# A fused S6, MoE, S5, MoE kernel: four small moves in its order by slots

## The reference, cut to what matters

```
x = x + S6(layernorm(x))       # 8 x 512 x 128; selective scan, 256 channels x 64 states
x = x + MoE(layernorm(x))      # 8 experts, hidden 256, top 2, all experts computed
x = x + S5(layernorm(x))       # diagonal complex scan, 64 states
x = x + MoE(layernorm(x))      # the same weights again

S6:   h[t] = exp(delta[t] * A) * h[t-1] + (delta[t] * x[t]) * B[t];  y[t] = C[t] * sum(h[t])
MoE:  logits = x @ Wg; the two largest, softmax over them -> combine
      out = sum_e combine[e] * ((silu(x @ W1[e]) * (x @ W2[e])) @ W3[e])
S5:   xs = scan with Lambda_bar = exp(Lambda * step); y = Re(C xs) + D * u
```

## Time and profile before

| | |
|---|---|
| device time, median of 3 runs | 1831.92 us (1828.08 to 1833.31) |
| the profiled execution | 1833.74 us, span 1831.9 us |
| mean granted TensorE clock | 0.866 |
| busy: VectorE, GpSimd, TensorE, ScalarE | 84%, 82%, 74%, 69% of the span |
| `h` scans on VectorE | 1024, mean 1210 ns, 1191.1 us busy |
| `w` products on GpSimd | 512, mean 2360 ns, 1192.4 us busy |

### The profile page before, as it was taken

How to read it: one execution, slowest core, us unless ns; L and a number is a source line. 1 busy time by engine, 2 the same in 40 slices (tenths; PEclk the granted TensorE clock), 3 DMA queues, 4 the chain that set the end, 5 groups by cost and what they waited for, 6 DMA issues and landing times. The chain is left out here.

```text
span 1831.9 us, 19041 instructions
## 1 busy us (share of the span) xinstructions
PE 1348.5 (74%) x5928; PEld 612.4 (33%) x5928; DVE 1535.7 (84%) x2154; ACT 1264.5 (69%) x2227; POOL 1497.5 (82%) x876
## 2 busy tenths in 40 slices
PE   5336468678866888778876887768876878668958
PEld 1001123234332433224332343324332343225525
DVE  3999988988899888998999888998999888995232
ACT  4558568777877678786886868777777777664413
POOL 0999989879998799978998899977998899984212
PEclk9556679888998989889897989989898989889969
DMA  3511411131113211122111310132101401100000
GB/s 117 192 52 50 165 46 52 50 123 67 58 47 104 89 52 52 49 92 98 58 46 56 137 52 29 55 109 98 50 32 50 164 29 49 46 29 1 6 1 6
DMA packets 38747, 121.89 MB, mean 67 GB/s; under 512 B 5875, under 2 KB 21110, under 8 KB 26358
## 3 DMA queue, kind: packets, MB, share of 16 engines
q1 hardware_dynamic: 37062, 120.67, 18.5%
q10 hardware_dynamic: 1584, 0.01, 0.0%
HBM read 109.13 MB, written 11.53 MB: 66 GB/s over the span
## 5 line engine op out<-in xcount | busy, mean ns | idle before, releaser
L1275 DVE TENSOR_TENSOR_SCAN h<-da,w 128x512 f32<-128x512 f32 x1024 | 1191.1, 1210 | 111.2 <-ACT da L853 94.5
L956 POOL TENSOR_TENSOR w<-ur,br 128x1024 f32<-128x1024 f32 x512 | 1192.4, 2360 | 29.9 <-DVE h L1275 17.5
L853 ACT ACTIVATE da<-dr,al 128x511 f32<-128x511 f32 x1024 | 680.8, 686 | 245.0 <-DVE h L1275 242.9
L646 PE MATMUL ys<-h,wsum 128*32 128x512 f32 x2048 | 315.4, 692 | 186.7 <-DVE h L1275 167.4
L580 PE MATMUL bankH<-nT,w 128*128 128x512 f32 x512 | 304.5, 679 | 98.5 <-DVE aq L1199 92.8
L899 POOL TENSOR_TENSOR x<-x,yk 128x512 f32<-128x512 f32 x120 | 152.5, 1271 | 181.4 <-ACT yk L815 181.4
L592 PEld LDWEIGHTS bankY<-w,aq 128*128 128x128 f32 x2048 | 250.6, 195 | 85.4 <-issue 75.8
L592 PE MATMUL bankY<-w,aq 128*128 128x128 f32 x2048 | 258.1, 280 | 12.4 <-DVE aq L1199 7.9
L580 PE MATMUL bankG<-nT,w 128*128 128x512 f32 x432 | 249.8, 662 | 16.4 <-DVE aq L1199 16.4
L815 ACT ACTIVATE yk<-bankY,rt 128x128 f32<-128x128 f32 x480 | 140.8, 360 | 86.6 <-PE bankY L592 77.5
L580 PEld LDWEIGHTS bankH<-nT,w 128*128 128x128 f32 x512 | 86.4, 203 | 258.0 <-DVE aq L1199 165.1
(11 more groups left out here) (188 smaller groups left out, 1156.0 us busy)
## 6 DMA issues: line engine op xcount, KB each, us to landing
br<-b_rows SPq DMA_DIRECT2D x64, 1024.0 KB, 5.0
dr<-d_rows SPq DMA_DIRECT2D x16, 1024.0 KB, 7.4
ur<-u_rows SPq DMA_DIRECT2D x16, 1024.0 KB, 8.4
d_rows<-vh SPq DMA_DIRECT2D x16, 256.0 KB
u_rows<-th SPq DMA_DIRECT2D x16, 256.0 KB
xnew<-in_L_attn_a_x_dram SPq DMA_DIRECT2D x8, 256.0 KB, 5.3
w<-in_L_ffn_W_dram SPq DMA_DIRECT2D x2, 1024.0 KB, 11.1
x<-in_L_attn_a_x_dram SPq DMA_DIRECT2D x8, 256.0 KB, 9.0
```

Of the source, the lines that this page charges most:

```text
L646: ins = nc.tensor.matmul(ys[32 * q:32 * q + 32, :], wsum[:, :], h[:, (DUOS * b + 2 * group + q // 2) % H_RING, q % 2, :], start=(n == 0), ...
L853: A(da[duo % D_RING][:, k % 2, 1:L], dr[:, half, q, 1:L], ACT.Exp, scale=nega[:, QUADS * half + q, n:n + 1]).then_inc(decay_ready, 1)
L956: G.tensor_tensor(w[:, turn_duo % W_RING, :, :], ur[:, half, q:q + 2, :], br[:, chunk % B_RING, row:row + 1, :].to_broadcast([128, 2, L]), ...
L1275: V.tensor_tensor_scan(h[:, turn_duo % H_RING, k % 2, :], da[duo % D_RING][:, k % 2, :], w[:, turn_duo % W_RING, k % 2, :], 0.0, ALU.mult, ...
```

## The change

Four moves of order; no instruction is added or taken away.

1. `x1T` goes from slot 26 in bank Y to slot 25 in bank G, and `h1_0` waits until it is drained.
2. `lg1` and `lg2` go a slot later (28 to 29, 105 to 106), and so do tiles `h_2` and `h_3` of both MoEs, so the logits stand behind `h_0` and `h_1`. R1 to R4 follow by their lags.
3. VectorE's S5 rotation, scan and rotation back go a slot later; TensorE's slots and line 1252's stay.
4. Ahead of turn 0 the S5 matrices are built (VectorE) and turned (TensorE) before `delta` is made, and the copy of the spread rows (line 1013) goes behind it.

```diff
+    if j in (2, 3) and step == 0:
+        return at + 1
...
-SETUP_ROWS_AT = PRE_AT + 9
-SETUP_AT = PRE_AT + 17
-MATRICES_AT = PRE_AT + 17
+SETUP_ROWS_AT, ROWS_AT = PRE_AT + 9, PRE_AT + 17
+SETUP_AT = PRE_AT + 11
+MATRICES_AT = PRE_AT + 10
...
-    (5, "post", "Y", "z"), (MOE_AT[1] - 2, "post", "Y", "x1T"), (MOE_AT[1], "post", "Y", "lg1"),
+    (5, "post", "Y", "z"), (MOE_AT[1] - 3, "post", "G", "x1T"), (MOE_AT[1] + 1, "post", "Y", "lg1"),
...
-    (MOE_AT[2] - 2, "post", "Y", "x3T"), (MOE_AT[2], "post", "Y", "lg2"),
+    (MOE_AT[2] - 2, "post", "Y", "x3T"), (MOE_AT[2] + 1, "post", "Y", "lg2"),
...
+                        if name == "h" and n == 0:
+                            pe.wait_ge(drained[BANK[turned]], t.before(turned) + 1)
...
+                yield ROWS_AT
                 v.wait_ge(rows_spread, 1)
                 chain(V.tensor_copy(bcs[:, :, :].rearrange("p n c -> p (n c)"), ys[:, 0:3 * D]))
...
-                yield SLOT["P1"] + 1
+                yield SLOT["P1"] + 2
                 p1, p2 = got(t, "P1"), got(t, "P2")
...
-                yield SLOT["P1"] + 5
+                yield SLOT["P1"] + 6
                 drain("P2", V.tensor_tensor(zt[1], p2[:, :], sinT[:, :], ALU.mult))
```

More of the change, by code:

```diff
@@ L167, in moe_pe @@
 def moe_pe(m, late):
-    return sorted(([] if late else [(MOE_AT[m], "lg", 0)]) + [(SLOT[f"h{m}_{j}"], "h", j) for j in tiles_in(m, late)]
+    return sorted(([] if late else [(SLOT[f"lg{m}"], "lg", 0)]) + [(SLOT[f"h{m}_{j}"], "h", j) for j in tiles_in(m, late)]
                   + [(SLOT[f"g{m}_{j}"], "g", j) for j in tiles_in(m, late)]
@@ L561, in moe @@
                 c = t.b - 1
-                lnk = {1: 2, 2: 4}[m]
+                lnk, turned = {1: 2, 2: 4}[m], f"x{2 * m - 1}T"
                 if not is_late:
@@ L1237, in post @@
                 V.tensor_tensor(p2[:, :], p2[:, :], sinT[:, :], ALU.mult).then_inc(sin_ready, 1)
-                yield SLOT["P1"] + 2
+                yield SLOT["P1"] + 3
                 v.wait_ge(drained[BANK["P1"]], t.before("P1") + 1)
@@ L1241, in post @@
                 V.tensor_tensor(p2[:, :], zt[2], p2[:, :], ALU.add).then_inc(turned_ready, 1)
-                yield SLOT["P1"] + 3
+                yield SLOT["P1"] + 4
                 v.wait_ge(turned_ready, c + 1)
                 V.tensor_tensor_scan(p2[:, :], rT[:, :], p2[:, :], 0.0, ALU.mult, ALU.add).then_inc(diagonal_scanned, 1)
-                yield SLOT["P1"] + 4
+                yield SLOT["P1"] + 5
                 v.wait_ge(diagonal_scanned, c + 1)
                 V.tensor_tensor(zt[0], p2[:, :], cosT[:, :], ALU.mult).then_inc(real_ready, 1)
-                yield SLOT["P1"] + 5
+                yield SLOT["P1"] + 6
                 drain("P2", V.tensor_tensor(zt[1], p2[:, :], sinT[:, :], ALU.mult))
```

## The result

The changed kernel takes 1878.26 us (median of 4 runs, 1877.65 to 1878.66) against 1832.62 of the kernel before (4 runs, 1828.08 to 1842.61): ratio 1.0241, 95% interval 1.0199 to 1.0283. The forecast was 1850.7 and its range ended at 1857. It is slower, as forecast, but by 46 us in place of 19.

The account below looks back on a forecast made before the run. Neither VectorE nor GpSimd is full; a turn's length is VectorE's work plus its waits. Terms 0 + 6.3 - 0.7 + 11.2 + 2.0 + 0 = +18.8 gave a median of 1850.7, range 1832 to 1857.

Parts of the forecast that it names:

- the first claim: Whole turn: a wait saved or added on VectorE carries through; 2.3 of the 2.8 us between turns 5 and 6.
- Start: Ahead of turn 0: an earlier first scan only lengthens later waits for products; 0, bounds -5.2 and 0.
- a sign of being wrong: Start-up: GpSimd's first product ahead of 46 would show the forecast wrong.
- rival D: Start-up: the 5.2 us are kept, 1845.5, if the first product comes sooner; chance 0.04.
- Rotation: S5: waits of 1.0, 1.1 and 0.3 replace 1.43; +1.05 per turn, +6.3 over turns 1 to 6, -0.7 in turn 7.
- Second MoE, start: Second routing, turns 1 to 7: tiles end 0.9 later and R3 adds 0.7; 7 x 1.6 = +11.2.
- The wait at slot 109: Second MoE: sign of being right, this wait grown to over 2, with R3 right behind the following `aq`.
- R3's 0.7: Second MoE: R3 leaves the wait of 1.97, stands behind its scan and delays the next by 0.7 us per turn.
- First MoE: First routing: +0.65 in turns 2, 4, 6 and 0 in turns 1, 3, 5, 7; sum +2.0.
- The wait of 1.2 for a product at slot 30: First MoE: sign of being right, a new wait of about 1.2 where R1 had filled the gap.
- End: After turn 7: same work, earlier rows against later logits; 0, bounds -1 and +1.
- Rival E: Both routings: TensorE at full clock, -0.6 x 7 at the second MoE; 1828.9, not slower; chance 0.08.

Follow-up runs that it names:

- fill_gap3: The changed kernel with 3 matmuls of zero weights ahead of the first tile of the first MoE's fourth quartet: 1856.86 us, ratio 1.0133.
- only_start: The kernel before with only the S5 matrices made ahead of `delta`: 1839.95 us, ratio 1.0017.
- only_router: The kernel before with only the router's logits and tiles `h_2`, `h_3` a slot later in both MoEs: 1848.73 us, ratio 1.0097.
- no_router: The changed kernel with logits and tiles `h_2`, `h_3` put back where they were: 1821.46 us, ratio 0.9941.
- no_rotation: The changed kernel with S5's rotation put back where it was: 1856.24 us, ratio 1.0135.
- after_fills: The changed kernel with 18 matmuls of zero weights per turn in TensorE's idle times: 1855.94 us, ratio 1.0119.
- best_fills: The changed kernel with logits and tiles put back where they were, plus 18 matmuls of zero weights per turn: 1818.98 us, ratio 0.9915.
- before_fills: The kernel before with 18 matmuls of zero weights per turn in TensorE's idle times: 1807.44 us, ratio 0.9851.
- only_turned: The kernel before with only `x1T` in bank G at slot 25, the logits waiting until it is drained: 1819.63 us, ratio 0.9962.

## Why the prediction was wrong

The step that failed is the first claim, that a wait saved or added carries through a turn and that, therefore, the edits' own waits sum to the change. Nothing was put down for stages that no edit touches. Measured from the starts of VectorE's scans in the two profiled executions (0 to 127 in each turn), turns 1 to 7 summed, in us:

| part | forecast | measured |
|---|---|---|
| start, to the first scan of turn 1 | 0 | -3.1 |
| first MoE, its routing (scans 22 to 36) | +2.0 | +2.8 |
| first MoE behind it, to the last `y` (36 to 84) | 0 | +27.2 |
| S5 and the next entry's projections (84 to 106) | +5.6 | +5.6 |
| second MoE, its routing (106 to 118) | +11.2 | +7.3 |
| second MoE, second quartet (118 to 128) | 0 | +9.5 |
| scans 0 to 22, and behind the last scan | 0 | -4.9 |
| sum | +18.8 | +44.4 |

Where the edits stand they cost 15.7, not far from the 18.8 that was forecast. The miss is the 36.7 us in two stages that no edit touches, less 8.0 at start and end. The 27.2 are for the most part TensorE's half clock at the fourth quartet and `y1_6`: fill_gap3 takes 23 away there. Per turn they are 4.7 against the shorter kind of turn, 5.4 less 0.7 at the third quartet against the longer. The 9.5 have the same look: fill_gap3 has 2.76 at the second quartet in its turn 3 and 1.61 in its turn 4, with the same code, but no run takes this one away by itself. Point by point:

- **Start.** Right in its mechanism: the first scan comes sooner, and the waits for products behind it grow. In every profiled kernel without edit 4 the first scan starts 7.6 us behind the first product, and 2.6 in this one and in only_start; yet the first scan of turn 1 is 164.1 us behind the first product in only_start as before. The 3.1 us are another thing: the first product came 4 us sooner in this run, named as a sign of being wrong and as the condition of rival D, and the edit doesn't explain it. It starts at 42.4 in only_router, which has no such edit, and at 45.7 in before_pad; over the 20 profiled kernels it lies between 42.3 and 46.8, and the kernel before is the latest of them.

```profile
42.73 18.61 POOL L960 TENSOR_TENSOR w<-ur,br 128x1024 f32<-128x1024 f32 x8 [12.35 <-issue]
...
45.31 34.60 DVE L1280 TENSOR_TENSOR_SCAN h<-da,w 128x512 f32<-128x512 f32 x30 [2.31 <-POOL w L960]
...
110.16 4.64 DVE L1280 TENSOR_TENSOR_SCAN h<-da,w 128x512 f32<-128x512 f32 x4 [2.41 <-issue]
```

- **Rotation.** Right in its mechanism: the wait of 1.43 became three, forecast as 1.0, 1.1 and 0.3, though ScalarE waits 3.31 for `C1` where I held on to 2.6.

```profile
1433.02 1.22 DVE L1280 TENSOR_TENSOR_SCAN h<-da,w 128x512 f32<-128x512 f32 x1 [0.92 <-ACT da L857]
...
1438.20 1.22 DVE L1280 TENSOR_TENSOR_SCAN h<-da,w 128x512 f32<-128x512 f32 x1 [1.06 <-ACT da L857]
...
1440.83 1.23 DVE L1280 TENSOR_TENSOR_SCAN h<-da,w 128x512 f32<-128x512 f32 x1 [0.28 <-ACT da L857]
```

  That is +0.8 per turn by the waits; from scan to scan it is +1.0 in the shorter kind of turn, +0.6 in the longer and +0.1 in turn 7, where -0.7 was forecast. That the total is 5.6 on the dot is in part luck. Alone the edit made no difference that can be told (0.9962 to 1.0013), below the +5.6 forecast, since other stages gave back what it cost.
- **Second MoE, start.** Mis-sized, 7.3 for 11.2. The wait at slot 109 was to grow over 2 and is 1.39. The waits are 1.50 (for the logits, a wait that was forecast to cost nothing) and 1.39 in place of 1.97, +0.9, and this holds R3's 0.7 already, since R3 no longer shortens the second of them. From scan to scan it is +1.0 per turn, not 0.9 + 0.7 = 1.6: R3 did add its 0.7, but the fourth tile ends 0.2 later behind scan 104 and not 0.9. The sum of states, priced at half rate, ran at full clock, 1.0 us from its start to the next:

```profile
1463.83 1.82 PE L584 MATMUL bankG<-nT,w 128*128 128x512 f32 x2
1465.58 1.06 PE L650 MATMUL ys<-h,wsum 128*32 128x512 f32 x8
1466.57 1.06 PE L576 MATMUL bankY<-wg,nT 128*128 128x8 f32 x8
...
1467.67 0.19 DVE L1175 TENSOR_REDUCE rc<-bankY 128x4 f32<-128x32 f32 x1 [1.50 <-PE bankY L576]
...
1472.19 1.22 DVE L1280 TENSOR_TENSOR_SCAN h<-da,w 128x512 f32<-128x512 f32 x1 [1.39 <-ACT da L857]
...
1490.94 1.22 DVE L1280 TENSOR_TENSOR_SCAN h<-da,w 128x512 f32<-128x512 f32 x1 [2.78 <-ACT da L857]
```

  The last row is the second quartet, where 1.42 became 2.78, +1.4 per turn, behind a `y2_0` that took 3.04 instead of 2.05. No term stood for it. From scan 118 to the end of the turn, only_router, no_router and no_rotation have at most 0.2 of it.
- **First MoE.** The sum is near (+2.8 for +2.0), but by luck. The wait of 1.2 for a product at slot 30 is there, and so is the wait for decays behind R2, in turns 2 to 7, and not in three:

```profile
1336.58 1.22 DVE L1280 TENSOR_TENSOR_SCAN h<-da,w 128x512 f32<-128x512 f32 x1 [1.19 <-issue]
...
1342.13 1.22 DVE L1280 TENSOR_TENSOR_SCAN h<-da,w 128x512 f32<-128x512 f32 x1 [1.30 <-ACT da L857]
```

  Until the scan with the wait of 1.43 a turn takes 59.3 us; before, 59.7 and 57.4 in turns. So from scan 22 to 36 it is +1.9 in turns 2, 4 and 6, forecast +0.65, and -0.4 in turns 3, 5 and 7, forecast 0; turn 1 is 1.9 shorter. In turn 6 the fourth tile ended 1.2 later behind `z` than before, since the last two tiles ran at half rate, and R3's 0.7 came on top. Against edit 1 with 3 and 4 (no_router, 56.9) it is +2.4. Why the last two tiles don't start sooner than before is a bank: `h1_2` takes bank H behind ScalarE's SiLU of `h1_0`, and this waits for the table. In after_fills TensorE, at full clock, has the first two tiles and the logits done and then waits 1.58 for that SiLU, and its clock is at half again:

```profile
889.70 0.96 PE L577 MATMUL bankY<-wg,nT 128*128 128x8 f32 x8
892.24 2.08 PE L585 MATMUL bankH<-nT,w 128*128 128x512 f32 x2 [1.58 <-ACT tq L811]
894.11 1.70 PE L585 MATMUL bankG<-nT,w 128*128 128x512 f32 x2
```

  With the logits first, in best_fills, `h1_2` starts at the same 35.5 us behind `z` and at full clock. The two tiles sooner gain nothing.
- **End.** Forecast 0, and 4.8 us were gained. With the same code there, before_pad has 148.3 us behind its last `z` and before 151.9, so this end too takes several times; how much is the edits' stays open.
- **Rival E**, a full clock at both routings, was given 1828.9, from a sum over the turns of two kinds. As an effect it exists (before_fills, in part of its turns), but the change doesn't bring it: at the second routing the tiles start at a clock of 0.50 as before. No rival had the clock fall at an untouched stage, though turns 5 and 6 of the kernel before, alike in code, differ by just such a thing: between 35 and 40 us behind `z` the granted clock is 0.53 in the one and 0.84 in the other.

What is shown: the edits' own places together cost about what was forecast; the changed kernel's turns 2 to 6 have the same length and the same stretches at half clock; added work breaks this pattern; and a fill at one place takes its 3.8 us away and 23 us in all. What is only argued: that the 9.5 us of the second quartet are the clock's. What stays open: why the clock falls behind one idle time of 2.9 us and not behind another, why turns take the lengths of 208.2, 211.6, 215.0 and 218.45 so often, and how the 57 us of the router's edit in company, or the 48.5 between the two kernels with fills, split into the edits' own and the clock's.

## What to carry to other kernels

Where a pipeline repeats and TensorE has idle times of 2 us and more, price an edit as its own waits plus a spread for the clock at every later stage (here 37 us stood in stages that no edit touches), and don't add the results of edits made alone. Look first at whether the turns of the profile repeat in one or in several lengths, and at what differs between them. Filling TensorE's idle time with matmuls that add zero and fit in it, counted by their measured duration, was worth more (25 us) than any order tried; and tiles moved ahead of other work gain nothing if the next one's bank hangs on an engine that isn't sooner.

## What was not expected of the hardware

- One program has several times: only_turned 1816.8 to 1840.1, and the 7 to 25 runs of the kernel before that stood beside the experiments 1828 to 1843, with granted clocks of 0.866 to 0.857. The changed kernel, in its repeating turn, stayed within 1 us in its four runs. The Trainium skill (TensorE: Matmul & The Clock Gate, section "Part 1: The HAM clock gate") says that the number of matmuls at half rate varies between runs of one kernel. The two groups of only_turned agree: their granted clocks are 0.874 to 0.880 in the fast one and 0.859 to 0.863 in the other.
- More clock gives less time than its share says. before_fills raised the mean clock from 0.866 to 0.908, which is 0.042 x 1832 = 77 us at full rate, for 25 us; after_fills raised it from 0.849 to 0.890 for 22.
- A delay of 0.66 us in each of seven turns (before_pad) changed the kernel before by 0.07%, -0.10 to 0.25, or 1.3 us: less than the 4.6 us that were added, which lie at the interval's end.
